# A language-model tower on one core: the first four blocks written out in a new order

## The reference, cut to what matters

```
h = table[ids]                              # last four rows of the table replaced by extra
x = layernorm(h)
ct = concat(x shifted by one step, x)       # 1024 wide
z = sigmoid(relu(ct @ W_act.T))             # pairs (re, im)
m = cummax(|z|)                             # along the sequence
kv = running complex product of z / m       # along the sequence
r = sigmoid(relu(ct @ W_rec.T))
h = h + (kv @ W_val.T) * r ** 4
q = ternary(layernorm(h), 0.33)             # -0.5, 0, 0.5
h = h + q @ (ternary(W_ffn, 0.2) + variation).T
```

## Time and profile before

| | |
|---|---|
| three runs | 843.25, 845.85, 846.78 us, median 845.85 |
| profiled execution | 847.05 us, of which the span is 845.2 us |
| TensorE busy | 795.7 us, 94% of the span |
| VectorE busy | 725.9 us, 86% |
| ScalarE busy | 576.0 us, 68% |
| POOL busy | 137.0 us, 16% |
| mean granted TensorE clock | 0.982 of 2.4 GHz |
| DMA | 83.74 MB |

### The profile page before, as it was taken

How to read it: one execution, slowest core, us unless ns; L and a number is a source line. 1 busy time by engine, 2 the same in 40 slices (tenths; PEclk the granted TensorE clock), 3 DMA queues, 4 the chain that set the end, 5 groups by cost and what they waited for, 6 DMA issues and landing times.

```text
span 845.2 us, 12309 instructions
## 1 busy us (share of the span) xinstructions
PE 795.7 (94%) x4766; PEld 470.1 (56%) x4766; DVE 725.9 (86%) x1159; ACT 576.0 (68%) x574; POOL 137.0 (16%) x109
## 2 busy tenths in 40 slices
PE   1696987999999999999999999999999999999998
PEld 0453636456474746647474655647475564747443
DVE  6889689898989888888988888898888888895897
ACT  2478866778685867768586767858686776856660
POOL 5213301123120200203020020202011020000001
PEclk9798999899999999999999999999999999999999
DMA  8546421419372551909063370907248190712023
GB/s 305 100 144 155 88 62 38 94 44 172 54 174 51 114 111 66 159 1 223 2 134 92 87 138 6 219 1 159 66 100 125 41 184 1 158 18 76 1 76 124
DMA packets 152346, 83.74 MB, mean 99 GB/s; under 512 B 138352, under 2 KB 138480, under 8 KB 152288
## 3 DMA queue, kind: packets, MB, share of 16 engines
q1 hardware_dynamic: 145808, 63.04, 35.9%
q0 software_dynamic: 5392, 17.83, 8.2%
q10 hardware_dynamic: 1088, 2.10, 0.7%
HBM read 24.28 MB, written 16.78 MB: 49 GB/s over the span
## 4 chain that ended last, share of the span: by engine, by line
PE 73%; DVE 10%; ACT 6%; issue 2%; POOL 0%; DVEq 0%; ACTq 0%
PE bank L338 24%; PE bank L375 22%; PE bank L404 16%; PE bank L418 11%; DVE chain L700 3%; ACT x_hi L498 1%; DVE r L854 1%; DVE h L862 1%; ACT chain L635 1%; DVE stats L868 1%; DVE stats L752 1%; DVE chain L802 1%; DVE chain L830 0%; DVE chain L821 0%; ACT r L526 0%
## 5 line engine op out<-in xcount | busy, mean ns | idle before, releaser
L404 PE MATMUL bank<-wval_hi,kv 128*128 128x512 f16 x512 | 156.2, 382 | 7.3 <-DVE kv L837 6.8
L338 PE MATMUL bank<-xT_hi,wact_hi 128*128 128x256 f16 x768 | 117.6, 277 | 11.7 <-ACT r L571 4.9
L338 PE MATMUL bank<-xT_lo,wact_hi 128*128 128x256 f16 x768 | 118.0, 277 | 4.3 <-DMA xT_lo<-x_lo 4.3
L269 POOL DMA_INDIRECT h<-table,rows x64 | 92.3, 1442 | 170.4 <-DMA out<-h 130.4
L338 PE MATMUL bank<-xT_hi,wact_lo 128*128 128x256 f16 x768 | 118.1, 277 | 0.0
L375 PE MATMUL bank<-wrec_hi,xT_hi 128*128 128x512 f16 x384 | 99.4, 382 | 3.5 <-ACT bank L510 3.5
L375 PE MATMUL bank<-wrec_lo,xT_hi 128*128 128x512 f16 x384 | 99.1, 381 | 0.0
L375 PE MATMUL bank<-wrec_hi,xT_lo 128*128 128x512 f16 x384 | 98.5, 379 | 0.0
L404 PE MATMUL bank<-wval_lo,kv 128*128 128x512 f16 x256 | 97.8, 382 | 0.0
L418 PE MATMUL bank<-wffn_hi,qT 128*128 128x512 f16 x256 | 97.0, 379 | 0.0
L418 PE MATMUL bank<-wffn_lo,qT 128*128 128x512 f16 x256 | 97.0, 379 | 0.0
(11 more groups left out here) (105 smaller groups left out, 1330.3 us busy)
## 6 DMA issues: line engine op xcount, KB each, us to landing
out<-h SPq DMA_DIRECT2D x15, 1024.0 KB, 5.5
xs<-xo SPq DMA_DIRECT2D x16, 448.0 KB, 3.6
chain<-w_act SPq DMA_DIRECT2D x4, 512.0 KB, 5.6
h<-w_rec ACTq DMA_DIRECT2D x4, 512.0 KB, 7.5
h<-table,rows POOLq DMA_INDIRECT x64, 6.0
kv<-w_val SPq DMA_DIRECT2D x1, 1024.0 KB, 7.9
r<-w_ffn SPq DMA_DIRECT2D x1, 1024.0 KB, 9.9
h<-w_var POOLq DMA_DIRECT2D x1, 1024.0 KB, 6.3
```

Source lines behind the costliest of these rows:

```text
L269: pool.indirect_dma_start(h[:, j % SLOTS, t, :], None, table, bass.IndirectOffsetOnAxis(ap=rows[:, TT * j + t:TT * j + t + 1], axis=0),).t ...
L338: ins = pe.matmul(dst.rearrange("p (s t) -> p s t", s=NSEQ), wact[a][:, kind, k, c * P:(c + 1) * P], xT[i % 2][b][:, kind, :, k, :], start ...
L404: ins = pe.matmul(bank[t + 4 * (j == LAST)][:, :], kv[a][:, k // 2, k % 2, t * P:(t + 1) * P], wval[b][:, k, :], start=(n == 0), stop=(n = ...
```

## The change

Blocks 4 to 15 keep their order. For block 0 the first act product is issued kind by kind instead of pair by pair, without the 20 matmuls on constants ahead. The even tiles are gathered, measured and normalised first; three of the four tap sums of w_act go to POOL; w_rec is loaded as each part of w_act lands; the second gather is issued behind the powers for block 0. The low half weights are the last part of each kind there.

```diff
-            pe.wait_ge(s_nb, 1)
-            for n in range(WARM):
-                pe.matmul(bank[6][:, 0:SEQ], ones[:, 0:P // 2].bitcast(F16), ones[:, :].bitcast(F16),
-                          start=True, stop=True)
+            first_act_term(E, 0, 2, 2, s_ashare)
+            first_act_term(D3, 1, 4, 3, s_aps_odd)
+            first_act_term(D1, 0, 5, 4, s_aps_even)
             for i in range(NBLK):
-                act_shared(i)
-                act_rest(i, 0)
...
+                if i > 0:
+                    act_shared(i)
+                    act_rest(i, 0)
+                if i == 1:
+                    bound(VAL_W)
...
+            def first_act_term(kind, e, n_hi, n_lo, done):
+
+                for a, b in WEIGHT_LO_FIRST_BLOCK:
+                    if a == 0:
+                        pe.wait_ge(s_xT[kind][b], 16)
+                        pe.wait_ge(s_whi[ACT_W], n_hi)
+                    else:
+                        if kind == D1:
+                            bound(REC_W)
+                        pe.wait_ge(s_wlo[ACT_W], n_lo)
+                    for p in range(PAIRS):
+                        if kind == D3 and a == 0 and b == 0:
+                            pe.wait_ge(s_acopy, p + 1)
+                        act_part(0, p, kind, e, a, b, 0)
+                        ins = act_part(0, p, kind, e, a, b, 1)
+                        if a == 1:
+                            ins.then_inc(done, 1)
```

On POOL:

```diff
-                for t in range(TT):
+                for t in (0, 2, 1, 3) if j == 0 else range(TT):
...
             gather(0)
+            for k in range(KT - 1):
+                pool.wait_ge(s_wact[k], 16)
+                pool.tensor_tensor(by_k(act_sum)[:, k, :], two_tap(act_nat)[:, k, 0, :], two_tap(act_nat)[:, k, 1, :],
+                                   ALU.add).then_inc(s_tap, 1)
+            pool.wait_ge(s_ve_even, 1)
+            pool.tensor_tensor(rstd[:, 0:TT:2], ve[0][:, 0:TT:2], half[:, 0, 0:TT:2], ALU.pow).then_inc(s_rstd_even, 1)
+            pool.wait_ge(s_ve[0], 1)
+            pool.tensor_tensor(rstd[:, 1:TT:2], ve[0][:, 1:TT:2], half[:, 0, 1:TT:2], ALU.pow).then_inc(s_rstd, 1)
             gather(1)
-            inverse_std(0)
             for k in range(KT):
                 pool.wait_ge(s_wrec[k], 16)
+            pool.wait_ge(s_lo[D1], 1)
...
                 if i == 0:
                     pool.wait_ge(s_wlo[REC_W], 3)
+                    pool.dma_start(by_k(ffn_nat), w_ffn.rearrange("(k p) c -> p k c", p=P)).then_inc(s_wffn, 16)
+                if i == 1:
+                    pool.wait_ge(s_wlo[VAL_W], 1)
                     pool.dma_start(by_k(var_nat), w_var.rearrange("(k p) c -> p k c", p=P)).then_inc(s_wvar, 16)
                 if i == 2:
-                    pool.wait_ge(s_wlo[FFN_W], 1)
+                    pool.wait_ge(s_sign, 2)
```

```diff
-        val_nat = kv_both[:, :, :, :, :].rearrange("p n r c t -> p (n r c t)").bitcast(F32)
-        ffn_nat = r4[:, :, :].rearrange("p t d -> p (t d)")
-        var_nat = h[:, 4, :, :].rearrange("p t d -> p (t d)")
-        sign = q[:, :, :].rearrange("p t d -> p (t d)")
+        val_nat = q_both[:, :, :].rearrange("p n d -> p (n d)").bitcast(F32)
+        ffn_nat = h[:, 4, :, :].rearrange("p t d -> p (t d)")
+        var_nat = q_both[:, :, :].rearrange("p n d -> p (n d)").bitcast(F32)
+        sign = wffn[1][:, :, :].rearrange("p k c -> p (k c)")
```

VectorE's and ScalarE's lists for blocks 0 to 3 are written out call by call. Of VectorE's, from the weights of block 0 to kv_lo(2), cut to the places that were moved:

```diff
+            modulus_scan(0)
+            dve.wait_ge(s_steps, 16)
+            turns(0)
+            reduce_angle(0)
+            dve.wait_ge(s_wval, 16)
+            largest(amax[:, VAL_W:VAL_W + 1], val_nat, s_amax[VAL_W])
+            weight_scale(VAL_W)
+            parts(0)
+            weight_lo(VAL_W, 0, wval[1][:, :, :], by_k(val_nat), wval[0][:, :, :])
+
+            kv_lo(0)
+            norm_stats(2)
+            norm_bias(2)
...
+            h1_var(0)
+            norm_stats(3)
...
+            weight_lo(FFN_W, 0, wffn[1][:, :, :], by_k(var_nat), wffn[0][:, :, :])
+            thresholds(0)
+            dve.wait_ge(s_wlo[FFN_W], 1)
+            ternaries(0)
+            log_ratio(2)
+            largest_scan(2)
+            modulus_scan(2)
+            gates(1, 0)
+            gates(1, 1)
...
+            for t in range(TT):
+                final(0, t)
+            parts(2)
+            thresholds(1)
+            kv_lo(2)
```

More of the change, by code:

```diff
@@ new lines, in _ @@
+            act.wait_ge(s_sc[VAL_W], 4)
+            weight_hi(VAL_W, wval[0][:, :, :], by_k(val_nat))
+            kv_hi(0)
+            for n in range(TT):
+                z_sigmoid(1, n)
+            norm_odd(2)
+            z_square(1)
+            norm_even(2)
+            x_hi(2, E)
+            squares(0)
+            rec_copy(1, 0)
+            logarithms(1)
+            rec_copy(1, 1)
+            x_hi(2, D3)
+            x_hi(2, D1)
+            modulus_exp(1)
+            act.preload_act_table_set("sigmoid_and_others")
@@ new lines, in _ @@
+            rec_sigmoid(1, 0)
+            rec_sigmoid(1, 1)
+            tangent(1)
+            arctangent(1)
+            rec_sigmoid(1, 2)
+            rec_sigmoid(1, 3)
+            act_copy(2, 0)
+            act_copy(2, 1)
+            sines(1)
+            kv_hi(1)
+            for n in range(TT):
+                z_sigmoid(2, n)
+            z_square(2)
+            act.wait_ge(s_sc[FFN_W], 4)
+            weight_hi(FFN_W, wffn[0][:, :, :], by_k(var_nat))
+            squares(1)
+            rec_copy(2, 0)
@@ new lines, in _ @@
+            logarithms(2)
+            rec_copy(2, 1)
+            norm_odd(3)
+            norm_even(3)
+            x_hi(3, E)
+            modulus_exp(2)
+            act.preload_act_table_set("sigmoid_and_others")
+            tangent(2)
+            arctangent(2)
+            x_hi(3, D3)
+            x_hi(3, D1)
+            for n in range(TT):
+                rec_sigmoid(2, n)
+            act_copy(3, 0)
+            sines(2)
+            act_copy(3, 1)
+            kv_hi(2)
+            squares(2)
@@ new lines, in _ @@
+            x_lo(4, E)
+            odd_difference(4)
+            even_difference(4)
+            gates(2, 0)
+            log_ratio(3)
+            largest_scan(3)
+            modulus_scan(3)
+            x_lo(4, D3)
+            x_lo(4, D1)
+            gates(2, 1)
+            for t in range(TT):
+                h1_stats(2, t)
+            h1_var(2)
+            turns(3)
+            thresholds(2)
+            reduce_angle(3)
+            norm_stats(5)
+            parts(3)
+            norm_bias(5)
@@ L964, in _ @@
+            for t in range(TT):
+                final(1, t)
+            kv_lo(3)
+            for i in range(4, NBLK):
+                if i > 4:
                     for t in range(TT):
                         final(i - 3, t)
-                if has(i - 2):
-                    ternaries(i - 2)
-                if i == 2:
-                    weight_scale(FFN_W)
-                if has(i - 1):
+                ternaries(i - 2)
+                if i > 4:
                     kv_lo(i - 1)
-                if has(i + 1) and not first:
+                if has(i + 1):
```

539 lines of the change are left out of this document (306 added, 233 removed).

## The result

The changed kernel takes 839.44 us (median of 9 runs, 838.13 to 841.91), the kernel before in the same comparison 846.13 (9 runs, 843.25 to 846.78): ratio 0.9923, 95% interval 0.991 to 0.9936. It is faster by 0.8%, which can be told from no change, but far from the 829 forecast and outside the range of 824 to 838. The profiled execution's span fell from 845.2 to 837.6: 7.6 us instead of 17.0.

A forecast was written before the change was run, and what follows sets the result against it. TensorE, 94% busy, was taken to bound the kernel, with some 69 us lost, nearly all before the third value product; gains 5.2 + 8.1 + 3.2 + 0.5 = 17.0 us gave 829, range 824 to 838.

The forecast's parts named there:

- T: Time when TensorE takes the bound of w_rec in block 0: from 42.67 to 37.5 us, a gain of 5.2.
- small waits 0.3: Last item of the start's sum, up to the bound of w_rec: 0.3 us for TensorE's small waits.
- Rival 1: Start not early: low transpositions and shift queue behind second gather and w_rec's loads; gain 13.5, 832 us; chance 0.18.
- T to V0: From the bound of w_rec to value product 0's first matmul: 54.3 to 46.2 us, a gain of 8.1.
- Rival 2: Block 0's vector chain gets no shorter, so its 8.1 us gain is missing: 837 us; chance 0.12.
- V0 to V1: Between first matmuls of value products 0 and 1: 51.66 to 48.8 or less; gain taken 3.2 us.
- In the new order I find four that remain, 3.7: VectorE's waits between value products 0 and 1: four remain, 3.7 us together, against 6.6 before.
- V1 to V2: Between first matmuls of value products 1 and 2: 51.8 to 51.3 us, a gain of 0.5.
- Behind V2: After value product 2's first matmul: block 3's list, 47.9, stays under TensorE's 48.53 us, so nothing is lost.
- Rival 3: Waits in blocks 2 and 3 eat every gain, each block 5 to 8 us over the floor: about 846; chance 0.06.
- Rival 4: Without warming matmuls the clock stays at 0.50 through block 0's products: slower, 851 us; chance 0.04.
- The rule on POOL's taps: Only two-input VectorE instructions contend with POOL, so tap sums at the start cost 0; 3.4 us left in the range.

The follow-up runs named there:

- experiment 9: The changed kernel with the second gather issued behind POOL's sum of w_rec; 837.65 us, one run.
- experiment 4: The changed kernel with VectorE's statistics and bias of block 2 moved back ahead of kv_lo(0); 841.46 us, one run.
- experiment 2: The changed kernel with POOL's load of w_var and the third gather held until block 2's odd difference is made; 838.66 us, one run.
- experiment 3: The changed kernel with block 2's logarithms ahead of its first recursion copy on ScalarE; 834.77 us, one run.
- experiment 11: The changed kernel with w_var and the third gather behind block 2's shift and block 2's logarithms ahead of its first copy; 834.25 us, median of 4 runs.

## Why the prediction was wrong

- **T (42.67 to 37.5; measured 39.16).** The first product's start held (19.9; 19.08). That the even kind was done at 27.6, forecast 27.8, is luck: 16 matmuls ran at half rate, not 25, which saved 1.0, but the low half that was to "land at 23 and hide" made TensorE wait 1.28. The step that failed is "small waits 0.3" in the odd kind: TensorE waited 1.54 there for the kind's own low half, which landed 8.0 us after its issue where the earlier trace rows has 3.9. Rival 1 had this mechanism; experiment 9, with the gather away, gives 3.1 or 4.4 per transposition, no wait and T at 36.0. It also shows that the term was badly cut: an earlier T that needs a later gather does not move V0.
- **T to V0 (54.3 to 46.2; measured 45.44).** Right in size and in mechanism: the load before the logarithms came at T + 15.8 (forecast 16.7), kv_lo is the last wait, and experiment 4 prices the moved statistics at 3.2. Rival 2 falls.
- **V0 to V1 (48.5; measured 50.88).** "In the new order I find four that remain, 3.7" missed a fifth wait, the 5.29 for the shift. I had costed w_ffn's load by when it is needed, not by what flies beside it, and w_var's load, whose new place is beside the shift, not at all. Without that company the forecast is met (48.37 in experiment 2, where VectorE's waits are 1.16, 1.27, 1.38 and 0.97). The "four" are only three by name; the fourth is the 1.16 for POOL's power. That the step stops near 48.5 is chance, though: VectorE's work there is 43.2, not the 45.1 that the sum leaves for it, its waits are 4.8 and not 3.7, and "less than 48.53 cannot be" was wrong. The first w_ffn product runs at 163 us in the kernel after, so V0 to V1 holds only 10.36 + 15.54 + 15.72 = 41.6 us of matmuls, and VectorE's chain, not TensorE, bounds this stretch.
- **V1 to V2 (51.3; measured 53.28).** At the full rate it is 51.6, as forecast within 0.3. The step that failed is the clause that half-clock matmuls after V1 "no longer count" (the prediction has it in the sum of V0 to V1): a gap of 2.45 us stood before V1, eight slow matmuls came behind it, and through the copy ahead of the logarithms their 1.7 reached VectorE. Experiment 3 shows that the 3.1 of these 51.6 above TensorE's 48.53 are the list's order and not the amount of work; the 1.7 stay (50.21).
- **Behind V2 (nothing lost; measured 3.9).** The largest miss: "Blocks from 4 on keep their order, so any time won at V2 stays to the end". They keep their order, but not what precedes it. I added up block 3's list (47.9) and stopped there; block 4's, which has to do the next x and the ternaries that block 3 no longer does early, has its clamps behind them, and from clamps to clamps that is 52.0 by the row. Rival 3 had waits of that kind for blocks 2 and 3, not for the joint.
- **Rival 4** fell: the first product ran at the full rate from 23.95 on. Its sign, a clock near 0.50 beyond 28 us, did show for short stretches: behind a gap of 2.15 the first eight or so matmuls of the recursion product ran at half rate, with a granted clock of 0.54 from 45 to 47 us. T to V0 met its forecast all the same.
- **The rule on POOL's taps.** Of the kernel after, POOL's timeline and VectorE's:

```profile
7.97 3.70 POOL L295 TENSOR_TENSOR chain<-chain 128x512 f32<-128x512 f32 x3
...
30.57 4.52 POOL L305 TENSOR_TENSOR h<-h 128x2048 f32<-128x2048 f32 x1 [5.71 <-DVE x_lo L896]
```

```profile
9.74 1.42 DVE L1072 BATCH_NORM_STATS2 stats<-h 128x6 f32<-128x512 f32 x2 [0.76 <-DMA h<-table,rows]
...
26.91 2.35 DVE L850 SCALAR_TENSOR_TENSOR wact_lo<-chain,wscale,wact_hi 128x2048 f16<-128x2048 f32 x1
...
30.31 3.46 DVE L830 TENSOR_REDUCE chunk_max<-h 128x1 f32<-128x1024 f32 x3
...
33.88 3.35 DVE L850 SCALAR_TENSOR_TENSOR wact_lo<-chain,wscale,wact_hi 128x2048 f16<-128x2048 f32 x1
```

Instructions with one input ran on: three maxima in 3.46 beside the large sum (30.57 to 35.09), two statistics in 1.42 beside the three tap sums (7.97 to 11.67) and 1.28 without them. The low part with two inputs took 3.35 beside the end of the large sum and 2.35 alone. The page "SBUF — State Buffer" of the Trainium skill, section "Who interferes with whom", held on both counts. So the taps cost nothing that shows, as taken, and the 3.4 us left in the range for them were not needed.

## What to carry to other kernels

Where a hand-written order meets a loop's, add up the list of the first block behind the joint as well, and look in it for the work that the old order had done a block earlier. A load that is "needed 25 us later" still costs whatever small transfer with a waiting engine flies beside it: before moving one, look who is on the way then. And in an in-order queue, put an instruction that waits for the bound engine behind the ones that feed the critical chain: the one moved line of experiment 3 won 3.1 us here, and with experiment 2's line 5.0 of the span, where the whole change had won 7.6.

## What the runs showed that I had not expected

- The profile's clock column and the durations disagree at the start. Busy time by stretch of the kernel after, at the first product and behind V1:

```profile
19.00:23.00 4.00, 3.60 (x16) 2.26 (x16) 3.94 (x5) 2.67 (x4) 3.09 (x3) 1.00 0.99 185
135.00:139.00 4.00, 3.52 (x9) 1.34 (x10) 3.93 (x16) 2.51 (x4) 1.27 (x2) 0.57 0.00 0
```

  In the first the granted clock is 1.00, while 16 matmuls took 3.60 us, twice the 1.91 of the later ones; in the second it is 0.57 and a matmul took up to 0.63 in place of 0.38. Twenty matmuls on constants, 4.43 us end to end up to 1.0 us before the first 16, did not change these.
- Whether matmuls behind a gap run at half rate is not set by the gap alone: behind 2.45 and 2.48 us before V1 eight did, behind 1.97 and 3.29 none, behind 3.30 (experiment 11) 14. With the old list of block 2 that alone moves V2 by 1.7 us (53.28 against 51.6).
- Transpositions and shifts beside a gather or a 1 MB load took up to 8.0 to 8.9 us to land (the three low transpositions of the change 3.2, 5.6 and 8.0, the shift of block 2 8.1 and 8.9), against 3.1 to 4.4 with the gather out of the way (experiment 9) and 3.2 and 3.4 for the shift alone (experiment 2).
